# The seam between two steps of a selective scan: gate product split around the projections, with two gate buffers

## The reference, cut to what matters

```
proj = h @ in_proj_w.T;  x, gate = proj[..., :1024], proj[..., 1024:]
u    = silu(causal depthwise conv of x, 4 taps, + conv_b)
p    = u @ x_proj_w.T;   dt, B, C = p[:, :128], p[:, 128:144], p[:, 144:]
delta = softplus(dt @ dt_proj_w.T + dt_proj_b)
h_t  = h_{t-1} * exp(delta_t * A) + (delta_t * u_t) * B_t     # 16 states
y    = sum_n h_t * C_t + u * D;   out = (y * silu(gate)) @ out_proj_w.T
```

## Time and profile before

| | us |
|---|---|
| median of 3 runs | 3786.78 (3784.57 to 3786.84) |
| profiled execution | 3784.98 |
| its span | 3783.2 |
| PE busy, DVE busy | 3307.2, 3288.1 |
| ACT busy, POOL busy | 2486.7, 2454.3 |

### The profile page before, as it was taken

One profiled execution on the slowest core, in us unless ns is written; L12 is line 12 of the kernel. 1 busy time (PEld: TensorE's weight loads), 2 busy tenths in 40 slices (PEclk: granted clock), 3 DMA queues, 4 the chain that ended last, 5 costly groups with the idle time before them and its releaser, 6 DMA issues.

```text
span 3783.2 us, 46308 instructions
## 1 busy us (share of the span) xinstructions
PE 3307.2 (87%) x12672; PEld 2362.4 (62%) x12672; DVE 3288.1 (87%) x6128; ACT 2486.7 (66%) x4790; POOL 2454.3 (65%) x1943
## 2 busy tenths in 40 slices
PE   5888984899999999999999999999999999985738
PEld 4666663675757676767666666666666666663515
DVE  5999882498989898989898989898989898989891
ACT  4777771376767685868676767676767676765650
POOL 0344442195959595959595959695959595957470
PEclk9999997999999999999999999999999999987868
DMA  2222213011111111211111111111111110101010
GB/s 100 67 78 77 83 61 119 20 36 34 41 35 40 34 41 33 43 34 40 35 40 35 40 36 40 34 40 35 39 37 42 32 47 29 52 22 35 21 36 6
DMA packets 119377, 165.36 MB, mean 44 GB/s; under 512 B 8544, under 2 KB 84192, under 8 KB 118624
## 3 DMA queue, kind: packets, MB, share of 16 engines
q1 hardware_dynamic: 119136, 162.63, 15.3%
HBM read 128.39 MB, written 25.69 MB: 41 GB/s over the span
## 4 chain that ended last, share of the span: by engine, by line
POOL 27%; PE 20%; DVE 18%; issue 15%; ACT 3%; DVEq 1%; POOLq 0%; DMA 0%; SPq 0%; ACTq 0%
POOL dBu L867 16%; POOL yacc L880 11%; DVE D L1309 10%; PE W L1065 7%; PE W L1115 6%; PE W L1138 2%; PE W L1097 2%; DVE prod L1328 2%; PE W L1142 2%; DVE D L1331 2%; PE D L1065 1%; DVE U L1260 1%; DVE yacc L1340 1%; ACT L917 1%; DVE hT L1222 1%
## 5 line engine op out<-in xcount | busy, mean ns | idle before, releaser
L1309 DVE TENSOR_TENSOR_SCAN D<-D,hc,dBu 128x256 f32<-128x256 f32 x2048 | 1437.2, 740 | 47.0 <-ACT D L1008 47.0
L867 POOL TENSOR_TENSOR dBu<-U,BC 128x512 f32<-128x512 f32 x1024 | 1294.1, 1275 | 277.1 <-DMA BC<-bc_scratch 190.1
L1065 PE MATMUL W<-nT,wffn 128*128 128x256 f32 x5632 | 1241.3, 382 | 47.1 <-ACT nT L906 32.6
L1065 PEld LDWEIGHTS W<-nT,wffn 128*128 128x128 f32 x5632 | 1058.6, 189 | 230.3 <-ACT nT L906 37.7
L1008 ACT ACTIVATE D<-delta,A 128x256 f32<-128x256 f32 x2048 | 891.6, 468 | 425.7 <-DVE yacc L1340 404.8
L880 POOL TENSOR_TENSOR yacc<-yacc,prod 128x512 f32<-128x512 f32 x736 | 934.1, 1269 | 262.8 <-DVE prod L1328 258.2
L1097 PE MATMUL W<-wffn,hT 128*128 128x512 f32 (+1 forms) x1408 | 640.5, 612 | 42.5 <-DVE hT L1222 42.5
L1097 PEld LDWEIGHTS W<-wffn,hT 128*128 128x128 f32 (+1 forms) x1408 | 273.0, 197 | 373.8 <-issue 322.8
L1328 DVE TENSOR_TENSOR prod<-D,BC 128x512 f32<-128x512 f32 x736 | 494.8, 672 | 0.0
L1065 PE MATMUL W<-nT,win 128*128 128x256 f32 x2048 | 453.8, 383 | 33.8 <-ACT nT L906 33.8
L1065 PEld LDWEIGHTS W<-nT,win 128*128 128x128 f32 x2048 | 391.3, 192 | 106.5 <-ACT nT L906 45.0
(11 more groups left out here) (118 smaller groups left out, 3211.4 us busy)
## 6 DMA issues: line engine op xcount, KB each, us to landing
BC<-bc_scratch SPq DMA_DIRECT2D x256, 256.0 KB, 4.6
XM<-x_scratch SPq DMA_DIRECT2D x29, 512.0 KB, 5.0
X<-x_scratch SPq DMA_DIRECT2D x17, 512.0 KB, 3.6
ix<-idx SPq DMA_DIRECT2D x33, 255.0 KB, 2.9
X<-x SPq DMA_DIRECT2D x16, 512.0 KB, 3.3
XR<-x SPq DMA_DIRECT2D x16, 512.0 KB, 3.4
x_scratch<-XR SPq DMA_DIRECT2D x16, 512.0 KB, 3.7
out<-X SPq DMA_DIRECT2D x16, 512.0 KB, 2.8
```

The lines of the kernel that those rows point to most:

```text
L867: nc.gpsimd.tensor_tensor(dBu[e % 4][:], U[:, 2 * j:2 * j + 2, :], BC[slot][:, 0:1, :].to_broadcast([P, 2, CH]), ALU.mult).then_inc(s_dBu, 1)
L1065: last = T_.matmul(dst, lhsT, rhs, start=(n == 0), stop=(n == len(terms) - 1))
L1309: V.tensor_tensor_scan(D[:, m, :], D[:, m, :], dBu[e % 4][:, m % 2, :], hc[:, n, m:m + 1], ALU.mult, ALU.add).then_inc(s_scan, 1)
```

## The change

- The gate product is split. Half 0 goes ahead of the wx products and writes W[0]; its silu follows in the seam. Half 1 goes behind wdt, into W[0] as well, with its silu at e = 3 (G_LATE).
- dt and B, C accumulate in two columns of D (4 and 6) and not in W[0]; wdt's column 6 waits for the copy of B, C.
- `project(i - 1)` is no longer split by FILL: its first row tile follows gate half 1, its second the turn. There are two buffers sgm, by the parity of the step.
- `gate_y(i - 1)` moves from the end of the loop into the seam, a half behind each two convolution groups. `out_resid(i - 1)` moves from ahead of the scan to e = 7.
- xext has all eight columns; the heads of the next chunk are written in place by one instruction (`heads`), and the buffer cc, four small copies and four small multiplies go. `taps` of columns 0 to 3 move into the loop's end, between the last saves.
- `skip` moves ahead of the dt copy. The places e of evacuations, silus, residuals and norms move, by two in steps with both blocks.

```diff
-FILL = 4
-G_SILU = (2, 5)
-F1_EVAC = G_SILU[1]
-F1_SILU = (12, 15, 18, 21, 24, 26)
-F2_STAT = 2
-F2_NORM = 26
-F1_RES = 33
-F2_EVAC = 34
-F2_SILU = (38, 41, 44, 47, 50, 52)
+G_LATE = 3
+F1_EVAC = 6
+F1_SILU = (10, 13, 16, 19, 22, 24)
+F2_STAT = 8
+RES_AT = 7
+F2_NORM = 24
+F1_RES = 31
+F2_EVAC = 32
+F2_SILU = (36, 39, 42, 45, 48, 50)
-M_STAT = 50
-M_NORM = 52
-M_EVAC = 59
-F2_RES = 58
+M_STAT = 48
+M_NORM = 50
+M_EVAC = 57
+F2_RES = 56
...
-        sgm = buf(ctx, "sgm", [ME, CH])
+        sgm = [buf(ctx, f"sgm{s}", [ME, CH]) for s in range(2)]
-        xext = [buf(ctx, f"xext{s}", [2, CH + KC - 1]) for s in range(2)]
-        cc = buf(ctx, "cc", [ME, KC - 1])
+        xext = buf(ctx, "xext", [ME, CH + KC - 1])
...
-            return dict(norm=F2_STAT + 1, evac=10, silu=(16, 19, 22, 25, 28, 30), res=38, m_stat=29, m_norm=31, m_evac=42)
+            return dict(norm=F2_STAT + 1, evac=14, silu=(18, 21, 24, 27, 30, 32), res=38, m_stat=29, m_norm=31, m_evac=42)
...
+                    def skip(j):
+                        act.wait_ge(m_u, 4 * i + j + 1)
+                        act.wait_ge(m_y, 2 * (i - 1) + j // 2 + 1 if i else 0)
...
+                    def gate_silu(h):
+                        act.wait_ge(m_g, 2 * i + h + 1)
+                        act.wait_ge(m_out, TT * max(i - 1, 0))
+                        N_.activation(sgm[i % 2][:, 4 * h:4 * h + 4, :], W[0][:], ACT.Silu).then_inc(m_sg, 1)
-                    taps(0)
-                    taps(1)
+                    taps(i, 2)
+                    taps(i, 3)
                     smooth(0)
-                    taps(2)
                     smooth(1)
-                    taps(3)
+                    gate_silu(0)
+                    skip(0)
+                    skip(1)
                     smooth(2)
                     smooth(3)
+                    skip(2)
+                    skip(3)
                     act.wait_ge(m_dt, i + 1)
-                    N_.activation(dtl[:], W[0][:, 0, :], ACT.Copy).then_inc(m_dtl, 1)
+                    N_.activation(dtl[:], D[:, 4, :], ACT.Copy).then_inc(m_dtl, 1)
                     act.wait_ge(m_bc, i + 1)
                     act.wait_ge(bc_stored, 16 * i)
-                    N_.activation(bcS[0:2 * S, :], W[0][0:2 * S, 2, :], ACT.Copy).then_inc(m_bcS, 1)
+                    N_.activation(bcS[0:2 * S, :], D[0:2 * S, 6, :], ACT.Copy).then_inc(m_bcS, 1)
...
-                    skip(0)
-                    skip(1)
-                    soft(0)
-                    soft(1)
-                    skip(2)
-                    soft(2)
-                    skip(3)
-                    soft(3)
+                    for j in range(ME // 2):
+                        soft(j)
...
-                        for h in range(2):
-                            if e == G_SILU[h]:
...
+                        if e == G_LATE:
+                            gate_silu(1)
...
-                    for e in range(NE - 4, NE):
-                        save(e)
+                    for j in range(4):
+                        save(NE - 4 + j)
+                        if more and j < 2:
+                            taps(i + 1, j)
...
+                    pe.wait_ge(m_tap, ME * i + 4)
+                    gate(0)
+                    pe.wait_ge(s_prod, NE * i)
+                    pe.wait_ge(s_ha, pool_sums(i))
                     for q in range(ME // 2):
-                        if back and q == 2:
-                            pe.wait_ge(m_tap, ME * (i + 1))
-                            project(i - 1, 0, 0, FILL)
...
-                            dt = T_.matmul(W[0][:, 0, :], wx[:, k, 0:R], U[:, k, :], start=(k == 0), stop=(k == ME - 1))
+                            dt = T_.matmul(D[:, 4, :], wx[:, k, 0:R], U[:, k, :], start=(k == 0), stop=(k == ME - 1))
...
                     for m in range(ME):
+                        if m == 6:
+                            pe.wait_ge(m_bcS, i + 1)
...
+                    pe.wait_ge(m_sg, 2 * i + 1)
+                    gate(1)
                     if back:
-                        project(i - 1, 0, FILL)
-                        project(i - 1, 1)
+                        pe.wait_ge(m_tap, ME * (i + 1))
+                        project(i - 1, 0)
...
-                    pe.wait_ge(m_sg, 2 * i + 1)
+                    pe.wait_ge(m_sg, 2 * i + 2)
                     if f1:
                         turn(L_, SIDE_EARLY)
-                        ffn(E_, L_, SIDE_EARLY, (m_sg, 2 * i + 2), L)
+                        if back:
+                            project(i - 1, 1)
+                        else:
+                            pe.wait_ge(m_tap, ME)
+                        ffn(E_, L_, SIDE_EARLY, (m_res, i), L)
...
+                def heads(i):
+                    dve.wait_ge(m_conv, 24 * (i + 1))
+                    V.tensor_scalar(xext[:, :, 0:KC - 1], xext[:, :, CH:CH + KC - 1], keep[:, i + 1:i + 2], None, ALU.mult).then_inc(m_cc, 1)
...
-                    for q in range(ME // 2):
-                        conv(i, q)
+                    for h in range(2):
+                        conv(i, 2 * h)
+                        conv(i, 2 * h + 1)
+                        if back:
+                            gate_y(i - 1, h)
...
-                    if back:
-                        out_resid(i - 1)
...
-                        if e == NE + 1:
-                            gate_y(i)
+                        if back and e == RES_AT:
+                            out_resid(i - 1)
...
-    nc = bacc.Bacc("TRN2", target_bir_lowering=False, num_devices=1)
+    nc = bacc.Bacc("TRN2", target_bir_lowering=False, num_devices=1, dynamic_dma_scratch_size=4096)
```

More of the change, by code:

```diff
@@ L1022, in step @@
                             norm(norm_no("M", i + 1), mamba_rows)
-                        for h in range(2):
-                            if e == G_SILU[h]:
-                                act.wait_ge(m_g, 2 * i + h + 1)
-                                act.wait_ge(m_out, TT * i)
-                                N_.activation(sgm[:, 4 * h:4 * h + 4, :], W[h][:], ACT.Silu).then_inc(m_sg, 1)
+                        if e == G_LATE:
+                            gate_silu(1)
                         if f1 and e == F1_EVAC:
@@ L1051, in _ @@
                 evac(1, 1 - SIDE_0)
-                act.wait_ge(b_setup, 3)
+                act.wait_ge(b_setup, 2)
+                taps(0, 0)
+                taps(0, 1)
                 steps_b(step, act)
@@ L1108, in ffn, with project @@
                     last.then_inc(f_out, 1)
-                def project(i, t, k0=0, k1=ME):
+                def project(i, t):
                     pe.wait_ge(m_y, 2 * (i + 1))
                     o = W[1][:].rearrange("p (t a) n -> p t (a n)", t=TT)
-                    for k in range(k0, k1):
-                        last = T_.matmul(o[:, t, :], sgm[:, k, t * P:(t + 1) * P], wo[:, k, :], start=(k == 0), stop=(k == ME - 1))
-                    if k1 == ME:
-                        last.then_inc(m_out, 1)
+                    for k in range(ME):
+                        last = T_.matmul(o[:, t, :], sgm[i % 2][:, k, t * P:(t + 1) * P], wo[:, k, :], start=(k == 0), stop=(k == ME - 1))
+                    last.then_inc(m_out, 1)
                 def first_product(i, free, h_free):
@@ L1129, in step, with gate @@
                 def step(i, back, f1, more):
+                    def gate(h):
+                        for m in range(4 * h, 4 * h + 4):
+                            last = chain(W[0][:, m % 4, :], [(win[:, k, E + m * P:E + (m + 1) * P], nT[:, k, :]) for k in range(KH)])
+                        last.then_inc(m_g, 1)
+                    pe.wait_ge(m_tap, ME * i + 4)
+                    gate(0)
+                    pe.wait_ge(s_prod, NE * i)
+                    pe.wait_ge(s_ha, pool_sums(i))
                     for q in range(ME // 2):
-                        if back and q == 2:
-                            pe.wait_ge(m_tap, ME * (i + 1))
-                            project(i - 1, 0, 0, FILL)
                         pe.wait_ge(m_u, 4 * i + q + 1)
                         for k in (2 * q, 2 * q + 1):
-                            dt = T_.matmul(W[0][:, 0, :], wx[:, k, 0:R], U[:, k, :], start=(k == 0), stop=(k == ME - 1))
+                            dt = T_.matmul(D[:, 4, :], wx[:, k, 0:R], U[:, k, :], start=(k == 0), stop=(k == ME - 1))
                         if q == ME // 2 - 1:
@@ L1235, in gate_y @@
                     dve.wait_ge(m_sg, 2 * (i + 1))
-                    for h in range(2):
-                        g = sgm[:, 4 * h:4 * h + 4, :]
-                        V.tensor_tensor(g, yacc[:, 4 * h:4 * h + 4, :], g, ALU.mult).then_inc(m_y, 1)
+                    g = sgm[i % 2][:, 4 * h:4 * h + 4, :]
+                    V.tensor_tensor(g, yacc[:, 4 * h:4 * h + 4, :], g, ALU.mult).then_inc(m_y, 1)
                 def out_resid(i):
@@ L1276, in step @@
                         shift(norm_no(*early(i)))
+                    if more:
+                        heads(i)
```

(6 more changed lines are left out.)

57 lines of the change are left out of this document (20 added, 37 removed).

## The result

The changed kernel takes 3648.32 us (median, 3645.19 to 3650.78), the kernel before 3786.81: a ratio of 0.9636, 95% interval 0.9621 to 0.965. The profiled execution of the changed kernel took 3647.6 us with a span of 3645.8, so 137.4 us have left the span. The forecast was 3658.

What follows compares the result with a forecast made beforehand. VectorE was taken to bound the scan loop, an engine-to-engine chain the seam. Thirteen steps at 9.5 us (123.5), two more seams and first- and last-step corrections gave -128.9 from 3784.98, hence 3656, median 3658 us; range 3643 to 3678.

Steps and rivals of the forecast that it cites:

- The seam: Stretch between two scan loops, a chain passing between engines: forecast to shrink from 34.2 to 27.3 us, 6.9 saved.
- the loop: Scan loop, bound by VectorE: forecast to go from 151.3 to 148.7 us, with 1.1 us of residual work added.
- rival (c): More than forecast: TensorE keeps its clock and the small waits go, 10.7 us a step, 3642 us; chance 0.14.
- small waits: Minor VectorE waits inside the scan loop, forecast to go and save 0.4 us a step.
- The 1.8 us that I had put on gate half 0 for the clock: Seam, TensorE: slow first records at the lowered clock add 1.8 us, gate half 0 running from -2.0 to 6.8.
- The residual at e = 7: Output projection's residual, moved into the loop: its 1.87 us wait goes, 1.14 us of work stays, 2 us of slack.
- Rival (a): First FFN keeps 4 us of stalls, VectorE waits 3.5 us at e = 31; step saving 6, 3704 us; chance 0.17.
- (b): Gate half 0 at the lower clock throughout: a step saves only 4.5 us, 3725 us; chance 0.07.
- (d): Slower: low clock outlasts gate half 0, covering projections and wdt; step 189.7 against 185.5 us, 3840 us; chance 0.04.
- sign of being wrong: Listed: VectorE waits over 1 us per step at L1228 or L1222, gate half 0 slow throughout, skips after last dt product.
- Rival (e): No effect: DMA or GpSimd sets the first scan's start anyway, time 3785 us; chance 0.03.
- the first scan's later start: First step: gate half 0 stands in the way with nothing to hide it, + 5.3 us (bounds 0 and 8).

## Why the prediction was right

**The step.** Forecast 176.0 us, measured 175.7; saved 9.5 forecast, 10.1 measured. The time lies in my own range of 3643 to 3678. The seam was forecast to lose 6.9 us and lost 8.2; the loop was forecast to lose 2.6 and lost 1.9. Both terms were off, with opposite signs: the seams brought 20 us more than forecast, the loops 9 us less. The mechanism was right in each, but that the sum came within 10 us of the measured time owes something to these two errors' cancelling. The measured 3648.3 lies between my forecast and rival (c) (3642, 10.7 a step), and so does its cause: TensorE kept its clock in six of the thirteen seams, about half of what (c) asked for, while most of the small waits stayed.

**Where the seam's term was short.** I took the seam of before from one step, into step 3, and its length is one of two that alternate: 34.9 and 36.0 us by the marks above, 20.9 and 22.0 of lead. In the trace of before the longer kind, into step 4, has three fours of wx records at 2.08, 1.92 and 1.94 us before they fall to 1.05; the sampled kind, into step 3, has two, 2.07 and 1.68, before 1.13. The mean is 35.5; half of the missing 1.3 us is that. The changed kernel also has two kinds, 15.8 and 16.8 of lead, and my 16.3 for L1286 (17.1 from the add) had taken the slow kind for all. Of the 0.8 us by which its mean of 16.3 is shorter, a bit over half is the seams at full clock; in the slow kind, gate half 0 and the projections were 0.3 us quicker than I had them. The 1.8 us that I had put on gate half 0 for the clock were 1.69 in that kind. So the mechanism was right, and the term that is mis-sized for the most part is the low clock, taken at one sample on either side.

**The loop's term.** Both waits for D, 1.85 and 1.48 us, are gone, as forecast, and the residual's 1.14 us came in. Of the small waits, which I had let go (0.4), the 0.2 us at the first FFN's residual went, while those of 0.36 us for nrm at L1227 are still there twice a step. Against that the records of the norms' statistics (L1213, L1218) take 0.7 us more in the step than before, which I had not counted. Less some 0.2 us that other records lost, the two make the loop's 0.7 us. I also named the waits for D at the fifth and the seventh pair; the first of them is at the fourth.

**Slacks.** The residual at e = 7: place forecast at T0 + 15.2, measured 15.1; project 1 forecast at T0 + 13.0, the FFN behind it began at 12.8. The experiment at e = 5 shows that this slack is real and no larger. TensorE's gap before gate half 0: forecast 3 us, measured 2.96. Rival (a), the first FFN missing its places, did not come: no wait for the first FFN at its residual in the changed kernel. Rivals (b) and (d), gate half 0 at the low clock throughout and beyond (13.8 us), did not come either: it took 8.86 us at most in the seams into steps 1 to 14, and 10.2 us in the worst of all versions there, with the wx products behind it at full speed. One sign of being wrong did come: ScalarE's skips end after the last dt product, by 1.1 us, in the seams at full clock. It cost little, for VectorE's own queue would have held L1292 to within 0.36 us of its place there. Rival (e) did not come. GpSimd's timeline in the seam into step 4, against the earlier trace rows:

```profile
1450.11 1.27 POOL L865 TENSOR_TENSOR dBu<-U,BC 128x512 f32<-128x512 f32 x1 [6.39 <-DVE U L1304]
```

Its first product waits for VectorE at L1304, and not for the BC load.

**The rest of the sum.** In the bookkeeping of the marks: fifteen seams 123.5 us, loops 1 to 13 24.4, together 147.9; back go 5.2 for the first scan's later start (forecast 5.3), 1.9 for the first loop (not forecast), 3.3 for the last two loops (3.0 forecast), 0.1 in the tail: 137.4. The forecast 128.9 (its printed terms add up to 128.8) was short by 8.5 us, which is the seams: 15 x 8.2 against 15 x 6.9 is 20, less 13 x 0.7 for the loops and the 2 of the first loop and the ends. The 5.2 us had the right size and in part the wrong cause: I named gate half 0, and with it behind wdt alone the first scan came no earlier (753.4). It came back to 747.6 only when the smoothing also went ahead of the copies of columns 4 to 7 and the repeated column left the first step; the shares of the three were not measured one by one.

**What the table loads were worth.** By the rows before, a pair is 2.6 us of ScalarE; after, the load at 1455.54 is followed by the silu at 1456.84, 1.30 us later, and again there is no drain to be seen. The figure of the Trainium skill, ScalarE: Activation LUTs, What ACT_TABLE_LOAD costs, which has 1.38 us of drain on top, is not what these rows show; here nothing hung on it.

## What to carry to other kernels

A wait in front of a loop is worth what it looks like only if the next wait behind it is not pinned to the same late producer: ask for each wait that is removed when the next input of that queue arrives, and move that producer too. Work that is moved ahead of a critical chain costs next to nothing while another engine's queue is as long, and what it buys can lie far behind, where its result no longer competes. When a kernel repeats one step, sample the step at least twice in succession before a term is multiplied by fifteen.

## What the runs showed of the hardware

The granted clock of TensorE did not follow the length of a gap alone. Behind the same 2.96 us of idle time, gate half 0 (32 records) took 7.17 us in six of the changed kernel's seams into steps 1 to 13 and 8.86 in seven, mostly in turn. The windows of two of them in succession, with the columns of the earlier trace rows (x33 and x34, for they touch a neighbour's record):

```profile
1427.57:1434.74 7.17, 7.17 (x33) 6.34 (x34) 6.93 (x17) 5.36 (x10) 1.27 (x1) 1.00 0.00 1
1603.10:1611.96 8.86, 8.86 (x33) 7.55 (x34) 8.62 (x20) 5.52 (x10) 1.27 (x1) 0.81 0.00 0
```

The granted clock was 1.00 in the first, which is 2.4 GHz all the way, and 0.81 in the second, which spent a part of its time at 1.2 GHz. In the version with the residual at e = 5, whose step is 3 us longer, the same gap was followed by 7.17 us twice, by 8.6 to 8.8 in six seams and by 10.1 (0.71 of the clock in step 4) in five. With a gap of 1.23 us gate half 0 took 7.17 us in all thirteen seams of each of four runs; with one of 6.24 us it took 8.6 to 10.1 (0.70 in step 4). What decides between the values behind one and the same gap these runs do not show. They do show its price: a version's time can move by 8 us with it, while the list of instructions and their waits give no hint. Filling the gap with a repetition of useful work, 1.75 us of TensorE, paid for itself.
